# Attention and FFN layer on one core: turned batches spread over the quarters, score copies shared by two engines

## The chip, the cores and the metric

One core of a Trainium2 chip runs the whole kernel. The metric is the device time of one execution in microseconds; lower is better. The engines are TensorE (PE, with its weight loads as PEld), VectorE (DVE), ScalarE (ACT), GpSimd (POOL) and SyncE (SP), which issues the DMAs.

## The reference

2048 tokens (4 x 512) of 1024 channels go through layer norm. The normalised rows feed two branches, whose results are added to the input. The first is an attention over heads: for each token, 32 heads of 32 channels attend to the 32 heads of the same token. The second is a gated FFN (3584 wide) with int4 weights scaled by group.

```python
q = (x @ Wq.T + bq).reshape(B, S, 32, 32)          # k and v alike
scores = einsum('bshd,bsgd->bshg', q, k) / sqrt(32)
scores = where(scores > 0.001, scores, -inf)
out = einsum('bshg,bsgd->bshd', softmax(scores), v).reshape(B, S, 1024) @ Wo.T + bo
ffn = (silu(x @ Wg.T) * (x @ Wu.T)) @ Wd.T
return x_in + out + ffn                             # x = layernorm(x_in)
```

## The kernel before

The tokens are cut into 16 tiles of 128. Up to about 80 us the three weight matrices are turned and split into a high and a low fp16 part, and tile 0 is projected. Then comes a loop over tiles, i = 1 to 16 (`tile_2`), and behind it the output projection and the FFN, which the change doesn't touch.

One pass of `tile_2(i)` does two things interleaved. It projects tile i (Q, K and V: six units u0 to u5 of 512 columns, each in four quarters of six matmuls, so 24 quarters s = 0 to 23), and it does the attention of tile j = i - 1. The table `STEPS` says which step of the attention follows quarter s on TensorE. All engines walk through the same table, each with its own part, and each engine's queue is strictly in this order:

- S0 to S3 (`scores`, L529): eight small matmuls each, scores of 32 heads against 32 for four tokens at a time. The wanted blocks lie on the diagonal of the result; four copies of 32 partitions x 256 (L784, ScalarE, with the scale) bring them out of PSUM into `s_c`. There are two pairs of banks: S2 waits for the copies of S0, and so on.
- X (`x_part`): the normalised rows of tile i+1 are split into a high part (ScalarE, L756) and a low part (VectorE, L975).
- R0 to R3 and T4 to T7 (`batch`, L513): eight transposes each. R turns the queries of tile i, T the values of tile i-1. They use two banks in turn (even ones the first, copied out by ScalarE, L774; odd ones the second, copied out by VectorE, L999). A batch waits until the last one but one is copied out: T6 for T4's copy, T7 for T5's, R0 of a tile for T6's of the tile before, which is done in the same pass.
- V0 to V3 (`head_products`, L546): probabilities times values. ScalarE copies the high part (L807), VectorE makes the low part (L1028). V2 waits for both of V0, V3 for those of V1.

Beside the table, fixed quarters hold the rest: VectorE's statistics of the next tile (`STATS_AT`), ScalarE's root (`ROOT_AT`, L750, with a load of the function table) and VectorE's normalisation (`NORM_AT`), the row maximum and its subtraction (`SHIFT_AT`, L1006 and L1010), the exponentials (`EXP_AT`, L790, ScalarE, with a table load), mask and sum (`MASK_AT`, L1014, L1017), reciprocal and product (`DIVIDE_AT`, L1021, L1023), and the split of the probabilities (`P_AT`: eight copies on ScalarE, L798, and eight subtractions on GpSimd, L1174), which SP's DMAs then turn. Behind each fourth quarter VectorE copies the finished unit out of PSUM (L992, `unit_copy`: the first thing it does in that quarter), ScalarE makes its high part twice (L768, the last thing it does in that quarter) and GpSimd its low part twice (L1174). R0 waits for the low parts of units 0 and 1. Within one quarter an engine does the steps of the table first, then the fixed items.

```python
STEPS = [["S0"], ["S1"], ["S2"], ["S3"], ["X", "T4"], ["T5"], ["T6"], ["T7"], [], [], [], [], ["R0"], ["R1"],
         ["R2"], ["R3"], [], ["V0"], ["V1"], ["V2"], ["V3"], [], [], []]
STATS_AT, ROOT_AT, NORM_AT, SHIFT_AT, EXP_AT, MASK_AT, DIVIDE_AT, P_AT = 0, 2, 2, 3, 4, 5, 6, 8
```

Of the kernel before, what the change touches and what calls it, by code (L numbers as in the profile page):

```python
# [32 lines left out]
ALU = mybir.AluOpType  # L33
ACT = mybir.ActivationFunctionType
# [7 lines left out]
def build(nc, x_in, Wq, bq, Wk, bk, Wv, bv, Wo, bo, gate_q, gate_s, up_q, up_s, down_q, down_s, out):  # L42
    B, S, H = x_in.shape
    T = B * S
    KT = H // P
    DH = 32
    NH = H // DH
    TG = P // DH
# [9 lines left out]
    INV_SQRT_D = float(np.float32(1.0 / np.sqrt(DH)))  # L58
# [10 lines left out]
    with ExitStack() as whole:  # L69
        def sem(name):  # L70
            return whole.enter_context(nc.semaphore(name))

        def sb(stack, name, shape, dt):
            return stack.enter_context(nc.sbuf_tensor(name, shape, dt))
# [8 lines left out]
        with ExitStack() as st:  # L83
# [11 lines left out]
            with ExitStack() as s2:  # L95
# [3 lines left out]
                s_c = sb(s2, "s_c", [P, GROUPS, DH], F32)  # L99
# [68 lines left out]
        batch_done = sem("batch_done")  # L168
        batch_out = [sem("batch_out_act"), sem("batch_out_dve")]
        s_done = sem("s_done")  # L170
        s_out = sem("s_out")
        row_max = sem("row_max")
        shifted = sem("shifted")
        exp_done = sem("exp_done")
        mask_done = sem("mask_done")
# [38 lines left out]
        def anchor(eng):  # L214
# [10 lines left out]

        STEPS = [["S0"], ["S1"], ["S2"], ["S3"], ["X", "T4"], ["T5"], ["T6"], ["T7"], [], [], [], [], ["R0"], ["R1"],
                 ["R2"], ["R3"], [], ["V0"], ["V1"], ["V2"], ["V3"], [], [], []]
        QUARTERS = len(STEPS)  # L230

        STATS_AT, ROOT_AT, NORM_AT, SHIFT_AT, EXP_AT, MASK_AT, DIVIDE_AT, P_AT = 0, 2, 2, 3, 4, 5, 6, 8

        LAST_UNITS = (QUARTERS - 2) // 2

# [29 lines left out]
        def steps_of(i, s):  # L265

            for name in STEPS[s]:
                kind, n = name[0], int(name[1:] or 0)
                if kind == "X":
                    if not isinstance(i, int) or i + 1 < TT:  # L270
                        yield kind, n
                elif kind == "R":
                    if projects(i):
                        yield kind, n
                else:
                    yield kind, n
# [12 lines left out]
        def projects(i):  # L289
            return not (isinstance(i, int) and i == TT)  # L290

        def wait_pos(eng, s, value):

            if not isinstance(value, int) or value > 0:
                eng.wait_ge(s, value)
# [4 lines left out]
        def pair(n):  # L300
            return psum[:, 4 + 2 * n:6 + 2 * n, :].rearrange("p b c -> p (b c)")
# [14 lines left out]
        def s_pair(k):  # L316
            return k % 2

        def v_pair(k):
            return (k + 1) % 2  # L320

        def block_of(k, r):

            src = pair(v_pair(k)).rearrange("p (g r a b) -> p r b a g", r=TG, a=KT, b=TG)
            return src[r * DH:(r + 1) * DH, r, :, :, :]
# [20 lines left out]
        def batch_dest(eng, j, m):  # L346

            if batch_matrix(m) == Q:

                wait_pos(eng, s_done, j * 4)  # L350
            else:

                wait_pos(eng, pv_done, j * 4)
            return turned[:, batch_matrix(m), :].rearrange("p (t x) -> p t x", x=NH)\
                [:, :, 8 * (m % 4):8 * (m % 4) + 8]

        def batch_source(m):
            return batch_bank(m).rearrange("p (x t) -> p t x", t=P)
# [113 lines left out]
        def _(pe):  # L472
# [43 lines left out]
            def scores(j, k):  # L516

                if k == 0:

                    pe.wait_ge(batch_out[0], j * 4 + 2)  # L520
                    pe.wait_ge(batch_out[1], j * 4 + 2)
                    pe.wait_ge(k_turned, j * 16 + 16)

                    wait_pos(pe, ctx_lo, j * 4)
                elif k >= 2:
                    pe.wait_ge(s_out, j * 4 + (k - 1))
                for n in range(8):
                    at = (8 * k + n) * P
                    last = mm(pair(s_pair(k))[:, n * P:(n + 1) * P], turned[:, Q, at:at + P],  # L529
                              k_turns[:, :, TG * (8 * k + n):TG * (8 * k + n + 1)], start=True, stop=True)  # L530
                last.then_inc(s_done, 1)

            def head_products(j, k):

                if k == 0:

                    pe.wait_ge(batch_out[0], j * 4 + 4)
                    pe.wait_ge(batch_out[1], j * 4 + 4)
                    pe.wait_ge(s_out, j * 4 + 4)
                elif k >= 2:  # L540
                    pe.wait_ge(ctx_lo, j * 4 + (k - 1))

                pe.wait_ge(p_turned[k], j * 16 + 16)
                for n in range(8):
                    at = (8 * k + n) * P
                    last = mm(pair(v_pair(k))[:, n * P:(n + 1) * P], turned[:, V, at:at + P],  # L546
                              probs_t[:, at:at + P], start=True, stop=True)
                last.then_inc(pv_done, 1)
# [188 lines left out]
        def _(act):  # L737
            run = nc.scalar.activation
# [37 lines left out]
            def scores_out(j, k):  # L776

                act.wait_ge(s_done, j * 4 + (k + 1))
                if k == 0:

                    wait_pos(act, mask_done, j)
                src = pair(s_pair(k)).rearrange("p (g h r) -> p g r h", r=TG, h=NH)
                for r in range(TG):
                    last = run(s_c[r * DH:(r + 1) * DH, 8 * k:8 * k + 8, :],  # L784
                               src[r * DH:(r + 1) * DH, :, r, :], ACT.Copy, scale=INV_SQRT_D)
                last.then_inc(s_out, 1)

            def exponentials(j):
                act.wait_ge(shifted, j + 1)
# [162 lines left out]
        def _(dve):  # L952
            v = nc.vector
# [19 lines left out]
            def x_part(i):  # L973
                dve.wait_ge(x_hi, i + 1)
                v.tensor_tensor(x_parts[:, LO, :], x_tile[:], x_parts[:, HI, :], ALU.subtract).then_inc(x_lo, 1)  # L975
# [11 lines left out]
            def unit_copy(i, u):  # L987

                dve.wait_ge(unit_done, i * 6 + (u + 1))

                wait_pos(dve, unit_lo, i * 6 + (u - 1))
                v.scalar_tensor_tensor(out=unit32[:, u % 2, :], in0=psum[:, u % 2, :], scalar=W_UNSCALE,  # L992
                                       in1=bias_qkv[:, u // 2, (u % 2) * BANK:(u % 2 + 1) * BANK],
                                       op0=ALU.mult, op1=ALU.add).then_inc(unit_copied, 1)

            def batch_copy(j, m):
                dve.wait_ge(batch_done, j * 8 + (m + 1))
                dst = batch_dest(dve, j, m)
                v.tensor_copy(dst, batch_source(m)).then_inc(batch_out[1], 1)  # L999

            def over_heads(ap):
                return ap.rearrange("p (g a) -> p g a", a=1).broadcast_to((P, GROUPS, DH))

            def softmax_shift(j):
                dve.wait_ge(s_out, j * 4 + 4)
                v.tensor_reduce(sums[:, 0, :], s_c[:], AX_X, ALU.max).then_inc(row_max, 1)  # L1006
                dve.wait_ge(row_max, j + 1)

                wait_pos(dve, p_lo, j * 4)
                v.tensor_tensor(p_c[:], s_c[:], over_heads(sums[:, 0, :]), ALU.subtract).then_inc(shifted, 1)  # L1010
# [21 lines left out]
            def wo_part(n2):  # L1032
                dve.wait_ge(wo_hi, n2 + 1)
                v.scalar_tensor_tensor(out=wo_half(LO, n2), in0=wo_bank(), scalar=W_SCALE, in1=wo_half(HI, n2),
                                       op0=ALU.mult, op1=ALU.subtract).then_inc(wo_lo, 1)

            def tile_2(i):
                more = not isinstance(i, int) or i + 1 < TT
                for s in range(QUARTERS):
                    if s % 4 == 3 and projects(i):  # L1040
                        unit_copy(i, s // 4)
                    if not projects(i) and s < 2 * KT:
                        wo_part(s)
                    for kind, n in steps_of(i, s):
                        if kind == "X":
                            x_part(i + 1)
                        elif kind == "R" and n % 2:
                            batch_copy(i, n)
                        elif kind == "T" and n % 2:
                            batch_copy(i - 1, n)  # L1050
                        elif kind == "V":
                            head_products_lo(i - 1, n)
                    if s == STATS_AT and more:
                        layer_stats(i + 1)
                    if s == NORM_AT and more:
                        layer_norm(i + 1)
                    if s == SHIFT_AT:
                        softmax_shift(i - 1)
                    if s == MASK_AT:
                        softmax_mask(i - 1)  # L1060
                    if s == DIVIDE_AT:
                        softmax_divide(i - 1)
# [439 lines left out]
```

## Time and profile before

| | us |
|---|---|
| median of 3 runs | 2157.17 (2156.26 to 2157.37) |
| profiled execution | 2158.44, its span 2156.5 |
| TensorE busy | 2034.0 (94%) |
| VectorE busy | 1581.5 (73%) |
| GpSimd busy | 1348.5 (63%) |
| ScalarE busy | 1253.2 (58%) |

The profile is of one execution. "Busy" is the time in which an engine had an instruction running. The span is that from the first instruction to the last. The timeline gives start and duration of instructions in order; neighbours of one kind on one engine are merged, with their count. The granted clock is the share of full speed that TensorE was allowed: 1.00 is 2.4 GHz, 0.50 is 1.2 GHz.

### The profile page before, as it was taken

To read this page: it belongs to the slowest core of one execution; us is meant where nothing else is said; L and a number is where in the kernel's file an instruction comes from. 1 tells how busy PE (TensorE), PEld (TensorE's weight loads), DVE (VectorE), ACT (ScalarE), POOL (GpSimd) and SP (SyncE) were. 2 spreads that over 40 slices of the span, in tenths; PEclk is the share of its full clock that TensorE was granted. 3 is DMA by queue.
4 is the path that set the end of the run, shared out by engine and by line. 5 is a ranking of instruction groups with operands and counts; after the bars stand their busy time and mean duration, and the time that the engine had idled before them with its cause. 6 is when DMAs were issued, how large, how long until landed. Compare 5 with 4: busy or idle time off the path is not lost. (4 is left out here: it accounts for less than half of the span.)

```text
span 2156.5 us, 36938 instructions
## 1 busy us (share of the span) xinstructions
PE 2034.0 (94%) x10880; PEld 973.1 (45%) x10880; DVE 1581.5 (73%) x1584; ACT 1253.2 (58%) x2017; POOL 1348.5 (63%) x769
## 2 busy tenths in 40 slices
PE   8899899989999899989999999999999999999996
PEld 5454445544554444424444444444444444444444
DVE  5565656565656420099999999899989998999897
ACT  4577666766676531226566665666566656565653
POOL 1344454445444200018888888888888888888886
PEclk9999999999999999999999999999999999999998
DMA  8354345444533536211122122112211221122118
GB/s 289 86 118 94 88 93 118 90 88 94 120 88 69 147 93 235 59 44 50 49 66 55 49 58 62 51 49 68 59 44 49 68 58 44 49 68 58 44 25 317
DMA packets 330006, 185.97 MB, mean 86 GB/s; under 512 B 269168, under 2 KB 306032, under 8 KB 329968
## 3 DMA queue, kind: packets, MB, share of 16 engines
q1 hardware_dynamic: 329968, 185.46, 33.0%
q8 instruction: 24, 0.39, 0.1%
q14 instruction: 14, 0.11, 0.0%
HBM read 96.29 MB, written 25.17 MB: 56 GB/s over the span
## 5 line engine op out<-in xcount | busy, mean ns | idle before, releaser
L644 PE MATMUL banks<-xt,lower 128*128 128x512 f16 x3584 | 861.7, 379 | 29.9 <-ACT lower L895 16.2
L1212 POOL TENSOR_TENSOR acc<-acc,lower 128x1024 f32<-128x1024 f32 x327 | 772.0, 2366 | 175.2 <-ACT lower L922 175.2
L922 ACT ACTIVATE lower<-banks,down_scale 128x512 f32<-128x512 f32 x654 | 413.8, 683 | 355.2 <-PE banks L669 263.6
L1099 DVE SCALAR_TENSOR_TENSOR lower<-banks,gate_scale,lower 128x1024 f32<-128x1024 f32 x392 | 479.2, 1277 | 146.2 <-PE banks L644 140.3
L644 PEld LDWEIGHTS banks<-xt,lower 128*128 128x128 f16 x3584 | 337.4, 98 | 486.5 <-DVE lower L1099 80.2
L499 PE MATMUL banks<-wt,xt_tile 128*128 128x512 f16 x2304 | 548.5, 383 | 4.2 <-ACT wt L743 2.6
L1099 DVE SCALAR_TENSOR_TENSOR lower<-banks,up_scale,lower 128x1024 f32<-128x1024 f32 x392 | 479.5, 1278 | 51.0 <-PE banks L644 44.9
L1174 POOL TENSOR_TENSOR stacks<-unit,stacks 128x512 f16<-128x512 f32 x192 | 247.0, 1307 | 375.9 <-ACT stacks L768 375.9
L669 PE MATMUL banks<-lower 128*128 (+1 forms) x1792 | 458.6, 380 | 4.6 <-DMA lower<-lower 4.4
L499 PEld LDWEIGHTS banks<-wt,xt_tile 128*128 (+1 forms) x2304 | 216.7, 99 | 220.1 <-issue 9.9
L669 PEld LDWEIGHTS banks<-lower 128*128 (+1 forms) x1792 | 175.4, 98 | 216.9 <-issue 17.1
L1218 POOL TENSOR_TENSOR lower<-lower 128x1024 f32<-128x1024 f32 x54 | 127.5, 2361 | 191.0 <-DVE lower L1099 191.0
L768 ACT ACTIVATE stacks<-unit 128x512 f16<-128x512 f32 x192 | 110.1, 621 | 131.6 <-DVE unit L992 128.8
L586 PE MATMUL banks<-lower 128*128 128x512 f16 x768 | 170.5, 382 | 3.4 <-ACT acc L820 2.6
L1028 DVE TENSOR_TENSOR ctx_parts<-banks,ctx_parts 32x256 f16<-32x256 f32 x256 | 107.4, 420 | 83.8 <-ACT ctx_parts L807 80.7
L1121 DVE SCALAR_TENSOR_TENSOR acc<-banks,down_scale,acc 128x1024 f32<-128x1024 f32 x106 | 135.6, 1279 | 22.3 <-PE banks L669 22.3
L999 DVE COPY turned<-banks 128x1024 f16<-128x1024 f16 x64 | 77.9, 1217 | 64.4 <-PE banks L513 64.4
L513 PE MATMUL banks<-ident,stacks 128*128 128x128 f16 x1024 | 80.3, 223 | 45.4 <-ACT turned L774 27.7
L807 ACT ACTIVATE ctx_parts<-banks 32x256 f16<-32x256 f32 x256 | 96.0, 375 | 45.1 <-PE banks L546 40.9
L1222 POOL TENSOR_TENSOR lower<-lower 128x1024 f32 (+1 forms) x54 | 115.5, 2139 | 2.1 <-ACT lower L909 2.1
L586 PEld LDWEIGHTS banks<-lower 128*128 128x128 f16 x768 | 74.8, 98 | 92.8 <-issue 6.5
L513 PEld LDWEIGHTS banks<-ident,stacks 128*128 128x128 f16 x1024 | 66.3, 100 | 86.9 <-ACT turned L774 34.8
(57 smaller groups left out, 1331.4 us busy)
## 6 DMA issues: line engine op xcount, KB each, us to landing
lower<-in_L_ffn_gate_q_dram SPq DMA_DIRECT2D x28, 512.0 KB, 3.6
lower<-in_L_ffn_up_q_dram SPq DMA_DIRECT2D x28, 512.0 KB, 4.4
lower<-in_L_ffn_down_q_dram SPq DMA_DIRECT2D x28, 512.0 KB, 3.9
x_tile<-in_L_attn_x_dram SPq DMA_DIRECT2D x16, 512.0 KB, 3.6
xt_scratch<-xt_tile SPq DMA_DIRECT2D x16, 512.0 KB, 2.8
ctx_scratch<-ctx_parts SPq DMA_DIRECT2D x64, 128.0 KB, 2.1
lower<-ctx_scratch SPq DMA_DIRECT2D x4, 2048.0 KB, 9.3
xt<-xt_scratch SPq DMA_DIRECT2D x4, 2048.0 KB, 15.6
```

The lines of the kernel that those rows point to most:

```text
L499: last = mm(psum[:, u % 2, :], xt_tile[:, :, :].rearrange("p a b -> p (a b)")[:, bass.ds(at, P)], wt[:, u // 2, wp, k, (u % 2) * BANK:(u % ...
L513: last = turn(batch_bank(m)[:, n * P:(n + 1) * P], stacks[:, mat, 8 * (m % 4) + n, :], ident16[:])
L586: last = mm(psum[:, output_bank(n), :], wo_t[:, wp, k, ho * P:(ho + 1) * P], ctx_t[c % 2][:, :, cp, k, :], start=(k == 0 and m == 0), stop ...
L644: last = mm(psum[:, 2 * (slot % 3) + c, :], gu_t[:, mat, g, :], xt[:, (2 * half + c) * CT:(2 * half + c + 1) * CT, part, g, :], start=(par ...
L669: last = mm(psum[:, bank, :], weights[:, bass.ds((t % 2) * (KT * P) + ho * P, P)], h_flat[:, bass.ds(at, BANK)], start=(part == HI), stop= ...
L922: run(down_tmp[:, buffer, c * BANK:(c + 1) * BANK], psum[:, 6 + c, :], ACT.Copy, scale=scale)\
L1099: v.scalar_tensor_tensor(out=acc_of[:, half, :], in0=gu_pair(slot % 3), scalar=scale[:, :, :].rearrange("p t k -> p (t k)")[:, bass.ds(t * ...
L1121: v.scalar_tensor_tensor(out=acc[:, half, ho, :], in0=gu_pair(slot % 3), scalar=down_scale[:, :, :].rearrange("p h t -> p (h t)")[:, bass. ...
L1174: return g.tensor_tensor(dst, src, hi, ALU.subtract)
L1212: g.tensor_tensor(acc[:, half, ho, :], acc[:, half, ho, :], down_tmp[:, buffer, :], ALU.add).then_inc(down_added, 1)
L1218: g.tensor_tensor(h_sb[:, half, :], h_sb[:, half, :], u_acc[:, half, :], ALU.mult).then_inc(h_done, 1)
L1222: g.tensor_tensor(h_part(t, half, LO), h_sb[:, half, :], h_part(t, half, HI), ALU.subtract)\
```

## The change

The turns of the values move from quarters 4 to 7 to quarters 5, 6, 9 and 10. V0 and V1 move one quarter ahead. The exponentials move from quarter 4 to 5, the mask from 5 to 7, the division from 6 to 7. The four copies of a group of scores are shared: blocks 0 and 1 by ScalarE, blocks 2 and 3 by VectorE, each with a semaphore of its own, and who waited for one semaphore now waits for both.

```diff
-        s_out = sem("s_out")
+        s_out = [sem("s_out_act"), sem("s_out_dve")]
...
-        STEPS = [["S0"], ["S1"], ["S2"], ["S3"], ["X", "T4"], ["T5"], ["T6"], ["T7"], [], [], [], [], ["R0"], ["R1"],
-                 ["R2"], ["R3"], [], ["V0"], ["V1"], ["V2"], ["V3"], [], [], []]
+        STEPS = [["S0"], ["S1"], ["S2"], ["S3"], ["X"], ["T4"], ["T5"], [], [], ["T6"], ["T7"], [], ["R0"], ["R1"],
+                 ["R2"], ["R3"], ["V0"], ["V1"], [], ["V2"], ["V3"], [], [], []]
...
-        STATS_AT, ROOT_AT, NORM_AT, SHIFT_AT, EXP_AT, MASK_AT, DIVIDE_AT, P_AT = 0, 2, 2, 3, 4, 5, 6, 8
+        STATS_AT, ROOT_AT, NORM_AT, SHIFT_AT, EXP_AT, MASK_AT, DIVIDE_AT, P_AT = 0, 2, 2, 3, 5, 7, 7, 8
...
+        def diagonal(k, r):
+
+            src = pair(s_pair(k)).rearrange("p (g h r) -> p g r h", r=TG, h=NH)
+            return src[r * DH:(r + 1) * DH, :, r, :]
+
+        def score_block(k, r):
+
+            return s_c[r * DH:(r + 1) * DH, 8 * k:8 * k + 8, :]
...
-                    pe.wait_ge(s_out, j * 4 + (k - 1))
+                    pe.wait_ge(s_out[0], j * 4 + (k - 1))
+                    pe.wait_ge(s_out[1], j * 4 + (k - 1))
...
-                for r in range(TG):
-                    last = run(s_c[r * DH:(r + 1) * DH, 8 * k:8 * k + 8, :],
-                               src[r * DH:(r + 1) * DH, :, r, :], ACT.Copy, scale=INV_SQRT_D)
-                last.then_inc(s_out, 1)
+                for r in (0, 1):
+                    last = run(score_block(k, r), diagonal(k, r), ACT.Copy, scale=INV_SQRT_D)
+                last.then_inc(s_out[0], 1)
...
+            def scores_out(j, k):
+
+                dve.wait_ge(s_done, j * 4 + (k + 1))
+                if k == 0:
+
+                    wait_pos(dve, mask_done, j)
+                for r in (2, 3):
+                    last = v.tensor_scalar(score_block(k, r), diagonal(k, r), INV_SQRT_D, None, ALU.mult)
+                last.then_inc(s_out[1], 1)
...
+                        elif kind == "S":
+                            scores_out(i - 1, n)
```

`head_products` and `softmax_shift` also wait for both semaphores instead of one.

## Rows read from the trace of the kernel before

**Rows 1.** The page, busy time of each engine over the whole span.
```profile
PE 2034.0 (94%) x10880; PEld 973.1 (45%) x10880; DVE 1581.5 (73%) x1584; ACT 1253.2 (58%) x2017; POOL 1348.5 (63%) x769
```
**Rows 2.** Waits, 60 to 760 us: who for whom, us in total, times, longest.
```profile
PE banks L513 <- ACT turned L774: 27.7, 15, 2.0
...
PE banks L513 <- POOL stacks L1174: 13.3, 15, 1.2
...
PE banks L546 <- DVE ctx_parts L1028: 6.3, 15, 0.4
```
**Rows 3.** Timeline of TensorE over one tile: start, duration, instruction, count, idle before.
```profile
336.28 0.61 PE L529 MATMUL banks<-turned 128*128 128x128 f16 x8
...
341.52 0.61 PE L529 MATMUL banks<-turned 128*128 128x128 f16 x8
...
348.88 0.73 PE L513 MATMUL banks<-ident,stacks 128*128 128x128 f16 x8 [1.97 <-ACT turned L774]
...
352.75 6.64 PE L499 MATMUL banks<-wt,xt_tile 128*128 128x512 f16 x30
359.62 0.62 PE L513 MATMUL banks<-ident,stacks 128*128 128x128 f16 x8 [0.23 <-POOL stacks L1174]
...
374.17 5.34 PE L499 MATMUL banks<-wt,xt_tile 128*128 128x512 f16 x24
379.35 0.61 PE L529 MATMUL banks<-turned 128*128 128x128 f16 x8
```
**Rows 4.** Timeline of ScalarE in the same tile.
```profile
337.74 4.66 ACT L784 ACTIVATE s_c<-banks 32x256 f32<-32x256 f32 x12
342.42 1.28 ACT L750 ACT_TABLE_LOAD   x1
...
347.80 1.02 ACT L774 ACTIVATE turned<-banks 128x1024 f16<-128x1024 f16 x1
...
350.14 1.06 ACT L790 ACTIVATE p_c<-p_c 128x1024 f32<-128x1024 f32 x1
351.10 1.01 ACT L774 ACTIVATE turned<-banks 128x1024 f16<-128x1024 f16 x1
...
357.04 2.54 ACT L798 ACTIVATE p_stack<-p_c 128x256 f16<-128x256 f32 x8
```
**Rows 5.** Timeline of VectorE in the same tile.
```profile
344.88 0.68 DVE L992 SCALAR_TENSOR_TENSOR unit<-banks,bias_qkv 128x512 f32<-128x512 f32 x1
345.51 1.22 DVE L1006 TENSOR_REDUCE sums<-s_c 128x32 f32<-128x1024 f32 x1
346.76 1.22 DVE L1010 TENSOR_TENSOR p_c<-s_c,sums 128x1024 f32<-128x1024 f32 x1
347.91 2.17 DVE L975 TENSOR_TENSOR x_parts<-x_tile,x_parts 128x1024 f16<-128x1024 f32 x1
350.00 1.21 DVE L999 COPY turned<-banks 128x1024 f16<-128x1024 f16 x1
...
354.13 1.22 DVE L1023 TENSOR_TENSOR p_c<-p_c,sums 128x1024 f32<-128x1024 f32 x1
```
**Rows 6.** Timeline of GpSimd in the same tile, low parts of units 0 and 1.
```profile
346.91 4.19 POOL L1174 TENSOR_TENSOR stacks<-unit,stacks 128x512 f16<-128x512 f32 x2 [6.84 <-ACT stacks L768]
357.21 2.27 POOL L1174 TENSOR_TENSOR stacks<-unit,stacks 128x512 f16<-128x512 f32 x2 [6.12 <-ACT stacks L768]
```
**Rows 7.** Timeline of VectorE and GpSimd in the last tile with projections.
```profile
689.78 2.20 DVE L1010 TENSOR_TENSOR p_c<-s_c,sums 128x1024 f32<-128x1024 f32 x1
...
689.75 3.25 POOL L1174 TENSOR_TENSOR stacks<-unit,stacks 128x512 f16<-128x512 f32 x2 [5.15 <-ACT stacks L768]
```
**Rows 8.** Windows: from:to, length, TensorE's busy time (instructions), granted clock, DMA share, GB/s.
```profile
14.80:21.40 6.60, 5.17 (x18) 0.50 1.01 371
349.30:352.60 3.30, 3.30 (x16) 0.50 0.25 48
564.40:567.60 3.20, 3.20 (x15) 0.50 0.14 27
```

More of the change, by code:

```diff
@@ L538, in head_products @@
                     pe.wait_ge(batch_out[1], j * 4 + 4)
-                    pe.wait_ge(s_out, j * 4 + 4)
+                    pe.wait_ge(s_out[0], j * 4 + 4)
+                    pe.wait_ge(s_out[1], j * 4 + 4)
                 elif k >= 2:
@@ L781, in scores_out @@
                     wait_pos(act, mask_done, j)
-                src = pair(s_pair(k)).rearrange("p (g h r) -> p g r h", r=TG, h=NH)
-                for r in range(TG):
-                    last = run(s_c[r * DH:(r + 1) * DH, 8 * k:8 * k + 8, :],
-                               src[r * DH:(r + 1) * DH, :, r, :], ACT.Copy, scale=INV_SQRT_D)
-                last.then_inc(s_out, 1)
+                for r in (0, 1):
+                    last = run(score_block(k, r), diagonal(k, r), ACT.Copy, scale=INV_SQRT_D)
+                last.then_inc(s_out[0], 1)
             def exponentials(j):
@@ L1002, in over_heads @@
                 return ap.rearrange("p (g a) -> p g a", a=1).broadcast_to((P, GROUPS, DH))
+            def scores_out(j, k):
[5 more added lines that the diff above has]
+                last.then_inc(s_out[1], 1)
             def softmax_shift(j):
-                dve.wait_ge(s_out, j * 4 + 4)
+                dve.wait_ge(s_out[0], j * 4 + 4)
+                dve.wait_ge(s_out[1], j * 4 + 4)
                 v.tensor_reduce(sums[:, 0, :], s_c[:], AX_X, ALU.max).then_inc(row_max, 1)
```

## The prediction

> **What bounds the kernel now.** I read the page first. TensorE is busy 94% of the span [rows 1], so only its gaps, and whatever slows its clock, can be won or lost. The change touches nothing but the loop over token tiles (about 60 to 760 us), so the next view was the waits of that stretch. TensorE's own waits there are few and regular [rows 2]: 15 for ScalarE's copy of a turned batch (L774, 27.7 us), 15 for GpSimd's low parts (L1174, 13.3 us), 15 for VectorE's context parts (L1028, 6.3 us). So one tile, looked at closely, stands for all.
>
> The timeline of TensorE over one tile shows it [rows 3]. Times below are counted from the first matmul of S0, at 336.28. The next S0 is at 379.35: a tile takes 43.07 us. Four quarters of projection take 5.18 us (379.35 - 374.17), so a quarter is 1.295; S0 to S3 is 5.24 for three quarters and three blocks, so a block is 0.45. 24 quarters and 16 blocks make 38.3 us. The other 4.8 are lost at three places. T6 starts at 12.60 (348.88), where 10.48 was possible: 2.1 us, for ScalarE's copy of T4. Then the clock falls: from T6 to the first quarter behind T7 takes 3.87 us in place of 2.2, so 1.7. R0 starts at 23.34 (359.62) where the quarters end 0.4 earlier. From R0 to the next S0 are 19.73 us for 12 quarters and 8 blocks, 19.14 if nothing waits: 0.6 at V2.
>
> The reader should see that R0 is released by a chain that begins at S0 and hardly touches TensorE: ScalarE's copies of the scores with root's table load among them [rows 4], then an unbroken row of VectorE work from L992 to L1023 and the unit copy behind it [rows 5], then ScalarE's and GpSimd's parts of that unit, whose end (357.21 + 2.27 = 359.48) releases R0 [rows 3, 6]. TensorE's stalls before R0, the slow clock too, lie in the shadow of this chain. The time of a tile is the chain from S0 to R0 (23.34) plus TensorE's work from R0 to S0 (19.73).
>
> **The change, part by part.** I follow the chain through the new order.
>
> *Scores by two engines.* ScalarE now makes two copies of a group, 2 x 0.39 (12 took 4.66 [rows 4]) instead of four. VectorE gets eight tensor_scalar operations of 32x256 a tile, which the trace doesn't show. Its bounds are nothing and the 0.68 of the unit copy L992, which has twice the elements of a partition [rows 5]; I take 0.38, as on ScalarE. S2's block begins at 3.49 and is done at 4.15 (0.61 and the hand-over); ScalarE is through with its half at 4.9, at once goes to root, and from root's table load to VectorE's unit copy of unit 0 are 2.46 us as before (344.88 - 342.42). So that unit copy comes at 7.4, VectorE's half of S3 from 8.03 to 8.8, and the row maximum (L1006) at 8.85. Before it was at 9.23. The eight copies taken off ScalarE win only 0.4 us here, because layer norm's root and the unit copy stand in the same queue.
>
> *The port between VectorE and GpSimd.* GpSimd's parts of unit 0 took 4.19 us where those of unit 1 took 2.27 [rows 6], and x_part (L975) took 2.17 where L1010 took from 346.76 to 347.9 (between the starts in [rows 5]). They ran at the same time. In the last tile with projections L1010 took 2.20 when GpSimd had begun 0.03 us earlier [rows 7]. So in these pairs one waits for the other's whole instruction, in turn: four instructions, two of either engine, took 346.76 to 351.10, 1.09 each. (The Trainium skill, SBUF — State Buffer, "Who interferes with whom", says this is an exclusive lock taken by a VectorE operation with two SBUF inputs and by GpSimd, while a tensor_reduce never takes it; the trace agrees with the first half, and no row shows a reduction beside GpSimd.) In the new order GpSimd starts 2.03 after the unit copy (346.91 - 344.88), at 9.43; L1010 is due at 10.1 and finds it busy. The four go GpSimd, L1010, GpSimd, x_part, and end at 9.43 + 4 x 1.085 = 13.77. T5's copy on VectorE starts there; before it started at 13.72 (350.00). The gain of 0.4 is gone. It also makes the price of the new VectorE operations free here: up to 0.6 each, L1010 would not come later than GpSimd's first end at 10.5.
>
> *Mask and divide moved behind the copy of unit 1.* From T5's copy to L1023 are 4.13 us (354.13 - 350.00) and the unit copy adds 0.61 (from L992's start to L1006's): L1023 is due at 18.5. The exponentials don't delay it: T4 is copied by ScalarE from 10.4, and from that copy's start to the end of exp were 3.4 us (347.80 to 351.20), so they end at 13.8, the mask starts at 15.6. But the unit copy at 15.0 now releases GpSimd's parts of unit 1 about 2.0 later, from 17.0 to 19.25, and L1023, with two SBUF inputs, meets the second of them. By the turn-taking above it starts at 19.2 and ends near 20.4; were the two not to meet, at 19.7. I take 20.4.
>
> *T6 and T7 at quarters 9 and 10.* TensorE no longer waits at T6 (its turn there is 14.35; T4's copy is out by 11.5), nor at T7. But on ScalarE the copy of T6 now stands behind the eight prob_hi parts of quarter 8, which wait for L1023. Before, it was at 351.10, ahead of them. And R0 may not write its bank before T6's copy is out: `batch` waits for `batch_out[0] >= 4 i`. So R0 waits for 20.4 + 2.5 (the parts, 2.54 [rows 4]) + 1.0 (a copy) = 23.9. TensorE without waits would be there at 12 quarters and 8 blocks, 19.14. The stalls that were spread over T6, T7 and R0 become one of 4.8 us ahead of R0. VectorE's copy of T7 (20.4 to 21.6), the copy of unit 2 behind it and GpSimd's prob_lo (21.1 to 26.2) are late as well, but are wanted only by R1, quarter 16 and V0 (about 31).
>
> *Turns of the values a quarter earlier for V0 and V1.* Between V1 and V2 there are now two quarters, so VectorE's parts of V0 are out (about 4.1 after V0 starts, V2 comes 4.8 after it): the 0.6 at V2 goes. SP's queue isn't held up: turn_probs can go from 22 on and has until V0, turn_k goes at 34 and has until the next S0 at 43.
>
> Without the clock the tile is then 23.9 + 19.14 = 43.05: the same as before.
>
> *The clock.* After T6's wait of 1.97 us the granted clock was 0.50, the 1.2 GHz level, for some 3.4 us in five of 15 tiles ([rows 8] shows two of the five), and it was at 0.50 through and after the 4 us wait of the opening, too. Before, this cost nothing: it lay ahead of R0. A wait of 4.8 us should bring it nearly every time, and what follows R0 is TensorE's own work, with no slack up to S0. If all the slow stretch falls on matmuls it costs the 1.7 worked out above; if some of it falls on the wait itself, less: with 1.2 us of it on the wait, 1.1. I take 1.35 a tile.
>
> **Sum.** 13 full tiles x 1.35 = 17.5. The first tile has no table load in its chain and gets about +1.6, the last one with projections about -0.3 (no norm: R0 at 20.9 instead of 20.6, V2's wait gone), the one with the output projection 0 ± 1. Together +19. The profiled execution took 2158.4 (span 2156.5), 1.3 above the median of 2157.2; the median after is then 2176.
>
> **Rivals.**
> *The chain gets short enough.* If reads at the port don't block in the new order, L1010 comes at 10.1, x_part at 11.25, T5's copy at 12.4, L1023 runs 17.15 to 18.35, R0 starts at 21.9, and a tile takes 41.0. With 1.35 for the clock it is 42.4, -0.7 x 14 = -9: 2148; if the clock holds in half of the tiles, 2138; in all of them, 2129. For it: ScalarE loses 3 us of work a tile. Against it: blocking shows in all tiles looked at. The forecast turns into a gain when R0 comes before 22.6. 0.22.
> *The clock stays up.* Then all is even: 2157 ± 4. Against it is that a wait of 2 us brought it down in a third of the cases. 0.10.
> *A larger loss.* Two slow stretches behind one wait (the opening has 6.6 us at 0.50 in one piece [rows 8]): +2.7 a tile, 2195. 0.10.
> *The change does what it is described to do and costs 1.1 to 1.7 a tile:* the forecast, 2165 to 2186. 0.58.
>
> The range: 2148 takes in the mild end of the first rival, 2192 most of the last. About 0.2% (4 us) can be told from no change here. Faster 0.22, same 0.10, slower 0.68.
>
> **What the profile after should show.** No wait at T6 and T7, none at V2; R0 waits 4.5 us or so each tile, released by ScalarE's L774 instead of GpSimd's L1174; R0 23.9 after S0 in the middle tiles; L1010 and L1023 at up to 2 us; a stretch with clock 0.50 at nearly every R0 and a tile near 44.4 us. New VectorE operations of 0.33 to 0.42. It would be wrong if L1023 ended before 19 (then R0 comes early), or if the clock stood at 1.00 behind R0.

## The result, and the profile after

The changed kernel takes 2180.67 us (median of 4 runs, 2180.13 to 2181.04), the kernel before 2157.27 on the same chips: ratio 1.0107, 95% interval 1.009 to 1.0125. It is slower by 23.4 us, as forecast (2176, range 2148 to 2192), by 4.7 more than the number given.

The page, beside [rows 1]: the span grew by 22.4. TensorE has the same work. ScalarE has lost 47 us of work and VectorE has gained 67, and the time is longer.

```profile
span 2178.9 us, 37001 instructions
PE 2036.2 (93%) x10880; PEld 980.6 (45%) x10880; DVE 1648.9 (76%) x1712; ACT 1206.2 (55%) x1889; POOL 1335.2 (61%) x769
```

The waits of TensorE, 60 to 760 us, answer to [rows 2]. Inside the loop the several kinds of wait have become one. GpSimd's low parts (L1174, now L1196) and VectorE's context parts no longer stop TensorE, and the waits for ScalarE's copy of a batch (L774, now L785) rose from 27.7 to 67.7 us. The second row belongs to the output projection.

```profile
PE banks L522 <- ACT turned L785: 67.7, 16, 4.7
PE banks L578 <- DVE lower L1054: 2.5, 2, 1.5
```

The timeline of TensorE over one tile, to be laid beside [rows 3]: S0 at 345.58, T4 at 353.86, T6 at 359.93, R0 at 369.55, V2 at 382.62. T6 and V2 are without a wait. All the waiting of the tile stands at R0, which starts 23.97 after S0, and the six matmuls behind R0 take 2.40 where others take 1.46.

```profile
345.58 0.61 PE L539 MATMUL banks<-turned 128*128 128x128 f16 x8
...
353.86 0.61 PE L522 MATMUL banks<-ident,stacks 128*128 128x128 f16 x8
...
359.93 0.61 PE L522 MATMUL banks<-ident,stacks 128*128 128x128 f16 x8
...
369.55 1.04 PE L522 MATMUL banks<-ident,stacks 128*128 128x128 f16 x8 [4.67 <-ACT turned L785]
370.38 2.40 PE L508 MATMUL banks<-wt,xt_tile 128*128 128x512 f16 x6
...
382.62 0.61 PE L557 MATMUL banks<-probs_t,turned 128*128 128x128 f16 x8
```

ScalarE in the same tile ([rows 4] before). In [rows 4] the copy of T6 stood at 351.10, right behind the exponentials; now it is the row at 368.49. T6 itself was over at 360.5; for 8 us its copy stands behind the row at 366.02, and that row waits 3.55 us for VectorE.

```profile
361.33 1.15 ACT L779 ACTIVATE stacks<-unit 128x512 f16<-128x512 f32 x2 [1.93 <-DVE unit L1001]
366.02 2.56 ACT L807 ACTIVATE p_stack<-p_c 128x256 f16<-128x256 f32 x8 [3.55 <-DVE p_c L1043]
368.49 1.00 ACT L785 ACTIVATE turned<-banks 128x1024 f16<-128x1024 f16 x1
```

VectorE and GpSimd in the same tile ([rows 5, 6] before). VectorE goes from one row to the next without a wait from 353.07 on. L1030 is L1010 of before, L984 is x_part, L1043 is L1023.

```profile
353.07 0.69 DVE L1001 SCALAR_TENSOR_TENSOR unit<-banks,bias_qkv 128x512 f32<-128x512 f32 x1
353.80 0.86 DVE L1020 TENSOR_SCALAR s_c<-banks 32x256 f32<-32x256 f32 x2
354.76 1.22 DVE L1026 TENSOR_REDUCE sums<-s_c 128x32 f32<-128x1024 f32 x1
356.02 1.33 DVE L1030 TENSOR_TENSOR p_c<-s_c,sums 128x1024 f32<-128x1024 f32 x1
357.27 2.17 DVE L984 TENSOR_TENSOR x_parts<-x_tile,x_parts 128x1024 f16<-128x1024 f32 x1
359.47 1.22 DVE L1008 COPY turned<-banks 128x1024 f16<-128x1024 f16 x1
...
362.46 1.22 DVE L1037 TENSOR_REDUCE sums<-p_c 128x32 f32<-128x1024 f32 x1
...
364.10 1.81 DVE L1043 TENSOR_TENSOR p_c<-p_c,sums 128x1024 f32<-128x1024 f32 x1
```
```profile
355.11 3.25 POOL L1196 TENSOR_TENSOR stacks<-unit,stacks 128x512 f16<-128x512 f32 x2 [5.97 <-ACT stacks L779]
362.56 2.27 POOL L1196 TENSOR_TENSOR stacks<-unit,stacks 128x512 f16<-128x512 f32 x2 [4.20 <-ACT stacks L779]
```

The second part of GpSimd's unit 1 runs to 364.83. L1043, issued at 364.10, takes 1.81 instead of the 1.22 of [rows 5], so it got through 0.6 late. The reductions L1026 and L1037, which also ran beside GpSimd, kept their 1.22.

Windows of the same trace, to [rows 8]. The first two lie at an R0 (325.11 and 369.55), the third runs from there to just before the next R0. The last is the second pass of the loop, whose R0 starts at 146.09 after a wait that began at 141.40: there the slow stretch is twice as long.

```profile
324.60:327.80 3.20, 2.69 (x13) 0.50 0.86 161
369.60:372.20 2.60, 2.60 (x13) 0.50 1.02 190
372.40:413.00 40.60, 36.88 (x260) 1.00 0.40 90
143.60:150.20 6.60, 4.11 (x21) 0.50 0.64 121
```

Where the 22.4 us of the span lie. S0 of the second pass is at 122.11 (before 120.95), S0 of the fifteenth at 700.63 (680.82), S0 of the last at 741.27 (721.93). The 13 passes between the first two took 578.52 instead of 559.87: +18.65, 1.43 a tile. The first pass gave +2.3 (43.42 for 41.09), and the part before its S0, which the change doesn't touch, -1.2 (78.69 for 79.86). The fifteenth pass gave -0.5. What is behind S0 of the last pass gave +3.1; that part includes the output projection and the FFN, which the change doesn't touch either.

### The profile page after: what moved, and what is told of

Read it like the earlier page. It is cut to its first block and busy times, and to the rows that moved or that the text cites. A ratio compares the mean times of both kernels' runs of the same rounds, so it can differ in the third digit from the quotient of the medians.

```text
span 2178.9 us, 37001 instructions
## 1 busy us (share of the span) xinstructions
PE 2036.2 (93%) x10880; PEld 980.6 (45%) x10880; DVE 1648.9 (76%) x1712; ACT 1206.2 (55%) x1889; POOL 1335.2 (61%) x769
## 5 line engine op out<-in xcount | busy, mean ns | idle before, releaser
L508 PE MATMUL banks<-wt,xt_tile 128*128 128x512 f16 x2304 | 555.7, 387 | 4.2 <-ACT wt L754 2.6
L1196 POOL TENSOR_TENSOR stacks<-unit,stacks 128x512 f16<-128x512 f32 x192 | 233.6, 1238 | 377.7 <-ACT stacks L779 377.7
L1143 DVE SCALAR_TENSOR_TENSOR acc<-banks,down_scale,acc 128x1024 f32<-128x1024 f32 x106 | 135.6, 1279 | 22.4 <-PE banks L680 22.4
L522 PE MATMUL banks<-ident,stacks 128*128 128x128 f16 x1024 | 84.2, 230 | 67.7 <-ACT turned L785 67.7
L1196 POOL TENSOR_TENSOR p_stack<-p_c,p_stack 128x256 f16<-128x256 f32 x128 | 81.0, 669 | 60.3 <-ACT p_stack L807 60.3
L522 PEld LDWEIGHTS banks<-ident,stacks 128*128 128x128 f16 x1024 | 71.6, 103 | 102.8 <-ACT turned L785 69.3
```

The source lines that it names most:

```text
L508: last = mm(psum[:, u % 2, :], xt_tile[:, :, :].rearrange("p a b -> p (a b)")[:, bass.ds(at, P)], wt[:, u // 2, wp, k, (u % 2) * BANK:(u % ...
L522: last = turn(batch_bank(m)[:, n * P:(n + 1) * P], stacks[:, mat, 8 * (m % 4) + n, :], ident16[:])
L1143: v.scalar_tensor_tensor(out=acc[:, half, ho, :], in0=gu_pair(slot % 3), scalar=down_scale[:, :, :].rearrange("p h t -> p (h t)")[:, bass. ...
L1196: return g.tensor_tensor(dst, src, hi, ALU.subtract)
```

## The experiments

Each ratio is to the kernel before on the same chip (medians 2157.5 to 2158.7). "A tile" is the time from one S0 to the next in the passes 2 to 14, which have the same code; S0, R0 and so on are given from the S0 of their tile.

**Scores shared, order of before.** The table `STEPS` and the fixed quarters go back to those of before.

```diff
-        STEPS = [["S0"], ["S1"], ["S2"], ["S3"], ["X"], ["T4"], ["T5"], [], [], ["T6"], ["T7"], [], ["R0"], ["R1"],
-                 ["R2"], ["R3"], ["V0"], ["V1"], [], ["V2"], ["V3"], [], [], []]
-        STATS_AT, ROOT_AT, NORM_AT, SHIFT_AT, EXP_AT, MASK_AT, DIVIDE_AT, P_AT = 0, 2, 2, 3, 5, 7, 7, 8
+        STEPS = [["S0"], ["S1"], ["S2"], ["S3"], ["X", "T4"], ["T5"], ["T6"], ["T7"], [], [], [], [], ["R0"], ["R1"],
+                 ["R2"], ["R3"], [], ["V0"], ["V1"], ["V2"], ["V3"], [], [], []]
+        STATS_AT, ROOT_AT, NORM_AT, SHIFT_AT, EXP_AT, MASK_AT, DIVIDE_AT, P_AT = 0, 2, 2, 3, 4, 5, 6, 8
```

> The scores are shared by the two engines, but the table and the fixed quarters are those of before. Theory 1 (the order costs, T6's copy behind the parts of the probabilities and then the clock): the row maximum starts 8.9 us after S0, GpSimd's parts of unit 0 meet L1010 first, T5's copy starts at 13.8 as before; R0 stays at 23.4 after S0, a middle tile at 43.1, time 2157 +- 3. Rival (the eight new operations on VectorE, whose queue is the chain, cost the time): a tile near 44.4, 2175 to 2181.

Measured: 2160.97 us, ratio 1.0016 (1.0006 to 1.0026), R0 23.41 after S0, a tile 43.15. That is the tile of theory 1, 0.08 longer than before; the time is 1.0 above its range. It is 3.5 over the kernel before. In the profile 1.1 of that are the 13 tiles, 0.7 is the later S0 of the first pass (80.56 for 79.86), and 2.4 lie behind the S0 of the last pass. So taking 3 us a tile off ScalarE and giving them to VectorE changes nothing for the better. The waits show how the same 4.8 us a tile are only dealt out anew: T6 waits less, and T7 more, for the copy of T5, which VectorE makes no earlier than before. Neither T6's wait (0.87) nor T7's (1.77) brought the clock down: it is 1.00 from 120 to 680 us.

```profile
PE banks L522 <- DVE turned L1008: 24.4, 14, 1.8
PE banks L522 <- POOL stacks L1196: 16.3, 15, 1.2
PE banks L522 <- ACT turned L785: 13.3, 14, 2.0
PE banks L557 <- DVE ctx_parts L1048: 6.2, 15, 0.4
```

**Order changed, scores by ScalarE.** The kernel before, with `STEPS` and the fixed quarters of the changed one (the diff above read the other way) and nothing else.

> The table and fixed quarters of the changed kernel, but all four copies of a group by ScalarE, as before. Theory 1: the row maximum is at 9.2, L1010 is now ahead of GpSimd's first part, T5's copy starts at 13.7 and all behind it is as in the changed kernel: R0 at 23.9, tile 44.4, 2181 +- 3. Rival (VectorE's new work costs): 2157 to 2165.

Measured: 2176.64 us, ratio 1.009 (1.0073 to 1.0107), 1.4 below the expected range; a tile 44.35, R0 at 23.56. The order carries the loss. R0 is 0.4 earlier than in the changed kernel, which I had not expected, and yet the tile is as long (44.38 there): from R0 to the next S0 it takes 20.79 here and 20.42 there. VectorE and GpSimd ahead of R0 (S0 at 388.33):

```profile
398.58 1.23 DVE L1010 TENSOR_TENSOR p_c<-s_c,sums 128x1024 f32<-128x1024 f32 x1
399.72 2.18 DVE L975 TENSOR_TENSOR x_parts<-x_tile,x_parts 128x1024 f16<-128x1024 f32 x1
401.83 1.21 DVE L999 COPY turned<-banks 128x1024 f16<-128x1024 f16 x1
```
```profile
398.73 4.20 POOL L1174 TENSOR_TENSOR stacks<-unit,stacks 128x512 f16<-128x512 f32 x2 [6.84 <-ACT stacks L768]
```

Here L1010 comes 0.15 ahead of GpSimd's first part and isn't held; T5's copy starts 13.50 after S0. With shared copies L1030 was issued 0.19 later (10.44 after S0 for 10.25) and GpSimd was first, by 0.9; T5's copy started at 13.89. So half of the 0.4 was there before the two engines met, and the other half came where they met.

**T6 one quarter earlier.** The changed kernel, one entry moved.

```diff
-        STEPS = [["S0"], ["S1"], ["S2"], ["S3"], ["X"], ["T4"], ["T5"], [], [], ["T6"], ["T7"], [], ["R0"], ["R1"],
+        STEPS = [["S0"], ["S1"], ["S2"], ["S3"], ["X"], ["T4"], ["T5"], [], ["T6"], [], ["T7"], [], ["R0"], ["R1"],
```

> The changed kernel with T6 one quarter earlier (8 instead of 9), so that ScalarE copies it before the eight parts of the probabilities and not behind them. Theory 1 (R0 waits for that copy): T6's copy is out by 18, R0 is released by GpSimd's parts of unit 1 at 19.3 after S0 instead of 23.97. Then R1 waits for VectorE's copy of T7 (21.6) and R2 for ScalarE's copy of R0 (25.0), which is behind the probabilities and unit 2. A tile is 25.07 + 15.65 = 40.7, with a little for the clock 40.7 to 41.5; time 2129 (2122 to 2140). Rival (R0 is held by the chain of VectorE, ScalarE and GpSimd as before, whatever T6 does): R0 stays above 22.5 and the time above 2160.

Measured: 2126.76 us, ratio 0.9857 (0.984 to 0.9873); a tile 40.65. One entry of the table turns 23 us lost into 31 won. ScalarE's queue shows how (S0 at 364.42): T6's copy now is at 381.23, in the gap in which ScalarE waits for VectorE anyway. The parts of the probabilities start 20.44 after S0, as in the changed kernel (366.02 - 345.58), so the chain ahead of them has not moved.

```profile
380.17 1.15 ACT L779 ACTIVATE stacks<-unit 128x512 f16<-128x512 f32 x2 [1.94 <-DVE unit L1001]
381.23 1.00 ACT L785 ACTIVATE turned<-banks 128x1024 f16<-128x1024 f16 x1
384.86 2.56 ACT L807 ACTIVATE p_stack<-p_c 128x256 f16<-128x256 f32 x8 [2.63 <-DVE p_c L1043]
...
388.37 1.00 ACT L785 ACTIVATE turned<-banks 128x1024 f16<-128x1024 f16 x1
```

TensorE starts R0 at 383.80, 19.38 after S0, without a wait. R2, at 389.42, waits 1.57 for the last row above, ScalarE's copy of R0:

```profile
383.80 0.62 PE L522 MATMUL banks<-ident,stacks 128*128 128x128 f16 x8
...
385.94 0.62 PE L522 MATMUL banks<-ident,stacks 128*128 128x128 f16 x8 [0.23 <-DVE turned L1008]
...
389.42 0.62 PE L522 MATMUL banks<-ident,stacks 128*128 128x128 f16 x8 [1.57 <-ACT turned L785]
```

**The wait filled with matmuls.** The changed kernel, with matmuls of no use ahead of R0 in every pass but the fifteenth; their bank is read by nobody.

```diff
+            def fill(i):
+
+                pe.wait_ge(s_out[0], (i - 1) * 4 + 4)
+                pe.wait_ge(s_out[1], (i - 1) * 4 + 4)
+                at = (i % 2) * (2 * KT * P)
+                for n in range(16):
+                    mm(psum[:, 4, :], xt_tile[:, :, :].rearrange("p a b -> p (a b)")[:, bass.ds(at, P)],
+                       wt[:, 0, HI, 0, 0:BANK], start=True, stop=True)
...
+                            if n == 0 and not (isinstance(i, int) and i == TT - 1):
+                                fill(i)
                             batch(i, n)
```

> The changed kernel with 16 extra matmuls of 128x512 ahead of R0 in each tile but the last with projections, into a bank that nobody reads (3.5 us of the wait of 4.7 are filled; the results are not used). Theory 1 (the wait itself costs nothing more than the chain, the slow clock behind it costs 1.3 to 2.1 us a tile, since R0 to S0 is TensorE's own work): the granted clock stays at 1.00 behind R0, R0 still at 23.97, a tile at 43.1; time 2180.7 - 14 x 1.35 = 2161 (2157 to 2164), although TensorE does more. Rival (the clock doesn't fall because of the wait, or its fall is hidden and something else stretches R0 to S0): 44.4 a tile, 2181 or more.

Measured: 2160.51 us, ratio 1.0014 (1.0004 to 1.0023), a tile 43.09. R0 is still 23.97 after S0 and still released by ScalarE's copy, and 3.5 us of added matmuls a tile make the kernel 20 us faster than the changed one. The clock is 1.00 over the tiles, and the wait that is left is 1.2 us:

```profile
120.00:680.00 560.00, 544.10 (x3745) 1.00 0.44 97
```
```profile
359.23 0.62 PE L531 MATMUL banks<-ident,stacks 128*128 128x128 f16 x8 [1.21 <-ACT turned L796]
```

That separates the two parts: the new place of the waits alone leaves the tile where it was (43.07 before), and the slow stretch that comes with a wait of 4.7 us is the 1.3 a tile.

**T6 at 8, scores by ScalarE.** The kernel before, with the table and the fixed quarters of "T6 one quarter earlier".

> T6 at quarter 8 as in the run before, but with all four score copies by ScalarE. In the two runs with T6 at 9 the row maximum came 9.2 after S0 with shared copies and 9.0 with ScalarE alone, R0 at 23.97 and 23.56. Theory 1 (sharing wins nothing, and its turn-taking with GpSimd costs 0.4 a tile): the probabilities, and with them R0's copy and R2, are 0.4 earlier; a tile at 40.25 in place of 40.65, time 2121 (2118 to 2124). Rival (once T6 is out of the way, ScalarE is what R2 waits for, so giving its work back costs): 41.5 or more a tile, above 2130.

Measured: 2119.77 us, ratio 0.9824 (0.9807 to 0.984), a tile 40.24. It is 7.0 us faster than with shared copies (8.1, each against the kernel before on its own chip); 0.41 x 13 = 5.3 of that are the tiles. Sharing the copies costs time in this order too.

**Late division.** Two lines changed against T6 at 8:

```diff
-                 ["R2"], ["R3"], ["V0"], ["V1"], [], ["V2"], ["V3"], [], [], []]
+                 ["R2"], ["R3"], [], ["V0"], ["V1"], [], ["V2"], ["V3"], [], []]
-        STATS_AT, ROOT_AT, NORM_AT, SHIFT_AT, EXP_AT, MASK_AT, DIVIDE_AT, P_AT = 0, 2, 2, 3, 5, 7, 7, 8
+        STATS_AT, ROOT_AT, NORM_AT, SHIFT_AT, EXP_AT, MASK_AT, DIVIDE_AT, P_AT = 0, 2, 2, 3, 5, 7, 11, 12
```

> Shared copies, T6 at 8, and the rest of the queues unblocked in the same way: the division at quarter 11 (behind VectorE's copies of T7 and unit 2), the parts of the probabilities at 12 (behind ScalarE's copy of R0), V0 to V3 at 17, 18, 20, 21. Theory 1 (what costs is a copy that TensorE needs standing behind softmax work): R0 at 19.4, R1 and R2 without a wait, V0 waits up to 0.7 for the turned probabilities; a tile 38.3 to 39.5, time 2107 (2100 to 2115). L1043 no longer meets GpSimd's unit 1 and takes 1.2 instead of 1.8. Rival (the softmax chain itself is too long for the tile, wherever it stands): the wait moves on to V0 and is as long as those before, 40.6 a tile, 2127.

Measured: 2137.07 us, ratio 0.9901 (0.9884 to 0.9917), a tile 41.18 to 41.31: a miss by 30 us. R0, R1 and R2 went as expected, L1043 took 1.22, V0 waited 0.5. But V2 and V3 had moved to quarters 20 and 21, and the expectation had no wait at the next S0. ScalarE makes the high parts of V3 behind those of unit 4 and V2, and VectorE's low parts come after them, 0.1 us before S0 starts, so S0 waited 1.9:

```profile
PE banks L539 <- DVE ctx_parts L1048: 26.1, 14, 1.9
PE banks L557 <- DMA probs_t<-p_stack: 7.9, 14, 0.9
```

> As the run before, with all four score copies by ScalarE. Theory 1: same or up to 0.4 a tile better than it, 2103 (2099 to 2112). Rival (the shared copies pay as soon as ScalarE's queue is short of time): 2112 or more, and slower than the run before.

Measured: 2135.38 us, ratio 0.9897 (0.9881 to 0.9914): the same wait at S0 (26.1 us in 14), a tile 41.38 on average. The forecast of 2103 missed for the same reason. The two versions can't be told apart by their times, and here the tile is 0.15 longer without sharing.

**Mask and division first.** T6 at 8, but `MASK_AT` and `DIVIDE_AT` both 6.

> T6 at 8, but mask and division at quarter 6, ahead of VectorE's copy of unit 1 (as in the kernel before) and not behind it. L1043 then meets no GpSimd work and takes 1.2. Theory 1: unit 1 is copied at 19.1 after S0 only, ScalarE does its part and then T6's copy (out at 21.9) ahead of the probabilities; GpSimd's parts of unit 1 end at 23.3 and release R0 there. A wait of 4.2 us, so the slow clock too: a tile 42.5 without it and 43.9 with it, time 2172 (2152 to 2176). So moving mask and division behind the unit copy was the useful part of the change. Rival (the collision with GpSimd is what costs): faster than T6 at 8 alone, below 2126.

Measured: 2178.3 us, ratio 1.0091 (1.0074 to 1.0108), a tile 44.21. L1043 meets nobody and takes 1.22, and still some 50 us are lost against the same kernel with 7 and 7 (19.6 over the kernel before, for 30.8 under it). TensorE waits twice, first at the projection of unit 3, which writes into unit 1's bank, then at R0:

```profile
PE banks L522 <- POOL stacks L1196: 30.6, 15, 2.1
PE banks L508 <- DVE unit L1001: 24.2, 14, 1.8
```

I had seen the second wait, not that the first takes half of it; the time was 2.3 above the expected range. The two waits are of 1.8 and 2.1 us, with 1.5 us of matmuls between them, and the clock fell to 0.50 in 12 of the 13 tiles. In the one in which it did not the tile took 42.53 in place of 44.21.

**V's back in place.** The late division with V0 to V3 at 17, 18, 19, 20.

> The late division with shared copies missed its 2107 (2137 measured), because S0 waited 1.9 us for VectorE's context parts of V3, which had been moved to quarter 21. Here V0 to V3 stand at 17, 18, 19, 20. Theory 1 (only V3's place was at fault): no wait at S0; V0 waits 0.5 for the probabilities, V2 0.6 for the parts of V0; a tile 39.6 to 40.0, time 2111 (2106 to 2117). Rival (the late division itself is too late: its work comes out at S0 wherever V3 stands): S0 waits on, a tile above 40.8, 2130 or more.

Measured: 2117.97 us, ratio 0.9813 (0.9797 to 0.9829), a tile 39.76 to 39.92. There is no wait at S0: the place of V2 and V3 was at fault. The time is 1 us above the range; the first pass was 41.0.

> As the run before, with all four score copies by ScalarE. Theory 1: a tile within 0.2 of it, time 2111 (2105 to 2117). Rival (sharing pays when the rest is short): more than 5 us slower than the run before.

Measured: 2113.36 us, ratio 0.9794 (0.9778 to 0.981), a tile 39.60 on average. It is the fastest version found: 44 us below the kernel before, 67 below the changed one. What is left a tile is 0.5 at V0 for the turned probabilities and 0.4 at V2:

```profile
PE banks L546 <- DMA probs_t<-p_stack: 7.3, 14, 0.7
PE banks L546 <- DVE ctx_parts L1028: 5.9, 14, 0.4
```

## Why the prediction was right

*R0 waits for T6's copy behind the probabilities.* Predicted 23.9 after S0 and a wait of 4.8; measured 23.97 and 4.67. Moving T6 alone brought R0 to 19.38, so this queue position is the cause and not the length of the chain, which was left as it was (the parts of the probabilities start at 20.44 in both).

*The clock.* Predicted at nearly every R0 and 1.35 us a tile. R0 to S0 took 20.42 in place of 19.14 in the middle tiles: 1.28. With the wait filled it was 19.12 (43.09 - 23.97) and the clock 1.00. The first tiles cost more, which I had not foreseen: the 45.19 of the second pass, 44.75, 44.61, 44.49, 44.43 shrank to 44.38. In the second pass the clock was at 0.50 for some 7 us. From the third on it was some 3.5 us each time; they began right at R0 in the third pass (about 191.2, R0 at 191.25) and 0.7 before it in the seventh (about 368.8, R0 at 369.55), so that less of them fell on matmuls. The sum was therefore 18.65 for 13 tiles and not 17.5. One premise was misread: the wait of 1.97 us stands in 13 tiles of the kernel before, not in 15, so the clock fell in five of 13. And 1.1 to 1.7 a tile doesn't give the 2165 to 2186 written beside it, but about 2173 to 2181 by the same sum.

*What the spread won.* T6, T7 and V2 lost their waits, the 0.6 at V2 among them. Without the clock this gives 23.97 + 19.12 = 43.09, against 43.05 predicted, and 43.09 is the tile measured with the wait filled.

*Shared copies free of charge, and of no use.* The row maximum came at 9.18, not 8.85: VectorE's unit copy was 0.1 later than predicted, its first copy of S3 another 0.1, and one such copy takes 0.43, not 0.38. T5's copy was at 13.89 (13.77 predicted). "Free of charge" was wrong in this order: without sharing T5's copy stands at 13.50 and R0 at 23.56, so sharing made R0 0.4 later. In the changed kernel that hardly shows in the tile (44.38 against 44.35), since with R0 at 23.56 the whole slow stretch lies behind R0 (about 412.0 to 415.4 with R0 at 411.88). That this came out even was luck. What sharing costs depends on the order: 0.08 a tile in the order of before, 0.41 with T6 at 8, 0.2 in the last two runs, and with V3 at 21 it wins 0.15.

*The turn-taking with GpSimd.* L1030 was held (1.33), x_part took 2.17 and L1043 1.81, ending 20.33 after S0 (20.4 predicted). Where L1043 meets nobody it takes 1.22 (late division, mask first). The Trainium skill, SBUF — State Buffer, "Who interferes with whom", says that a tensor_reduce never contends with GpSimd. The trace after agrees: L1037 ran from 362.46 beside GpSimd's parts from 362.56, and they took 1.22 and 2.27, as they do elsewhere.

*The rest, and the 4.7 us by which the number was short.* The tiles gave 1.1 more than predicted. The first pass gave +2.3 (+1.6 predicted), the fifteenth -0.5 (-0.3). The part before the first S0 gave -1.2 and the part behind the last S0 +3.1, where nothing and 0 ± 1 were predicted. The remaining 1.1 come from the profiled execution of before, which is 1.3 above its median where the one after is 0.1 above. That the total came out within 5 us is in part luck, since these terms have both signs. In the twelve profiles the first S0 stands anywhere from 78.0 to 80.9, although the code ahead of it is the same; from the last S0 to the end are 1434.6 us before and 1437.6 after, 1437.0 with shared scores in the old order, 1435.3 with the order alone and 1436.8 with the filled wait. What makes these 2 to 3 us wasn't tried and stays open.

The rival "the chain gets short enough" needed R0 before 22.6 and fell with 23.97; "the clock stays up" fell with the windows; "a larger loss" would have needed a doubled slow stretch in every tile, and there was one in the second pass alone (45.19, 2.1 over the 43.09 without a slow clock). The moves of V0 and V1 and of the exponentials were not tried by themselves.

## What to carry to other kernels

A step that is moved later on one engine drags its follow-up on another engine's queue with it: look at what it now stands behind there, and who waits for it. Here one copy of 1 us, behind softmax work that waited for VectorE, was worth 54 us, and the fix was one quarter. An engine relieved of work gains nothing if the chain's next step stands behind another engine's result in the same queue. Gathering several short waits into one long wait isn't neutral for TensorE: here the clock fell with the one wait of 4.7 us in every tile, and it also fell with two waits of 1.8 and 2.1 that stood close together. If the wait must be, it is best placed where slack follows, as T6's was before: the tiles in which the clock fell took 43.07 like the others.

## What was not expected of the hardware

Matmuls without use in a wait made the kernel 20 us faster (2160.5 against 2180.7), though R0 started not a hundredth of a microsecond earlier. After a wait of 1.97 us the clock had fallen in five of 13 tiles, with one of 4.67 in each. Waits of 1.57 us at most, in the run with T6 at 8, and of 1.77 us, in the run with shared scores in the old order, left it at 1.00 through 120 to 680 us. And a VectorE instruction that came 0.2 us later, with GpSimd now ahead of it where both read SBUF, moved everything behind it by 0.4.
